# A graph layer with two MLPs on one core: the linear product made first, its scaled rows the gather table

## The chip, the cores and the metric

One Trainium2 chip, one of its cores. The time is the device's, in microseconds, of the whole program; each kernel is run several times and the median is given. The engines are named TensorE (PE in the profile), VectorE (DVE), ScalarE (ACT), GpSimd (POOL) and SyncE (SP). All numbers are fp32.

## The reference

x is 3125 nodes of 256 features; there are 50,000 edges, sorted by destination, with a weight each.

```python
def gnn(features, src, dst, w, W, b):
    msgs = features[src] * w[:, None]
    agg = segment_sum(msgs, dst, 3125)
    return einsum('ni,oi->no', agg, W) + b

x = x + gnn(layernorm(x), src, dst, edge_weight, W, b)
x = x + ffn(layernorm(x))
```

`ffn` is a shared MLP of three layers plus the two best of four small expert MLPs, mixed by a softmax gate. Layer norm subtracts the mean of a row and divides by its deviation.

## The kernel before, in words

The nodes are 25 tiles of 128. At the start each tile of x is loaded (SyncE, line 599), its statistics are made on VectorE (1163), the deviation on ScalarE (758), and the tile is normalised into `xn_all`, three of four tiles on ScalarE (764), one on VectorE (1180). Each group of four tiles is then stored to a table `normalised_rows` in HBM (ScalarE's DMA queue, 739). There are seven groups, and all seven must have landed (`s_table`) before any row is read back.

The sums by destination are made in two ways.

For the first 19 tiles of nodes (units G0 to G10, one or two tiles each) the edges' source rows are gathered from HBM. A chunk is 128 edges. GpSimd issues one indirect DMA a chunk. 12 chunks are a batch, and there are 26 batches, 308 chunks. The first 24 chunks (2 batches, `RAW_BATCHES`) are gathered from x itself, so that they need not wait for the table (692); their rows are normalised in SBUF afterwards (751, 1322). The other 284 come from the table (708), into a ring of three batches. A slot of the ring is free when TensorE has used it (`s_used`). TensorE multiplies each chunk with a selector that VectorE makes (1356, 1360) into a window of 128 node slots (927), ScalarE copies the window (776), and `merge` puts windows in their places in the unit (945) with a placement matrix (1368).

For the last 6 tiles (units D0 to D2) no gather is needed: VectorE makes one-hots from the edges' records, 36 groups of them (1408, 1412), TensorE builds a dense adjacency (962), ScalarE copies it (786), and TensorE multiplies it with `xn_all` (974).

Either sum is features by nodes. ScalarE copies it (`sums`, 801), TensorE multiplies it with the weights W (`lin`, 990), VectorE adds x and the bias (1432) and makes the statistics (1436, 1440). Then a unit goes through std on ScalarE (807), norm (1451), turn (1001), logits and layer 1 (1011, 1025), the gates, layers 2 and 3 (1034 to 1070), `finish` (1544) and the store (652).

After a start that is written out by hand, the order of steps on each engine is made by `schedule()` at build time. It keeps a clock for each engine with assumed durations and picks among the steps that are ready by rank: `FIRST` for batches, `BUILD`, `MULT`, `BEHIND` for a younger unit. All three engines follow its lists, in order. ScalarE changes between a table with square root and one with exp, and each change is a load (ACT_TABLE_LOAD).

Line 700, GpSimd's branch on a flag, stands between the raw gathers and the others; so do branches on the other engines. The flag says that the edges fit the windows; with these inputs they do, and the other branch is never run.

## Time and profile before

| what | us |
|---|---|
| median of 3 runs | 438.74 |
| the three runs | 437.04, 442.10, 438.74 |
| the profiled execution, its own time | 436.16 |
| its span, first to last instruction | 434.4 |
| busy: TensorE / VectorE / ScalarE / GpSimd | 355.3 / 242.1 / 161.8 / 307.4 |
| mean granted clock of TensorE | 0.953 |

A row of the timeline gives start, duration, engine, line, operation, out<-in and how many were merged; in brackets the idle time of the engine before it and what ended it. "issue" means that the profile shows nothing that the engine waited for. A group's row gives its busy time, the mean of one, and the idle time of the engine before it. An fp32 matmul is two records in the profile, a transpose one. The granted clock is a share of 2.4 GHz; 0.5 is 1.2 GHz.

### The profile page before, as it was taken

The page shows a single profiled execution, that of the slowest core. Times are in us where ns is not written, and L with a number is a line of the kernel's source. Part 1 is how long each engine was busy: PE and PEld are TensorE (multiplying, and loading weights), DVE is VectorE, ACT ScalarE, POOL GpSimd, SP SyncE. Part 2 cuts the span into 40 slices and gives each one's busy share as a digit, 9 for nine tenths or more (in the row PEclk, how much of TensorE's full clock was granted, in tenths as well). Part 3 has the DMA queues.
Part 4 walks back from the last instruction along what each step waited for, and adds up shares of the span by engine and source line. Part 5 has one row for each costly group of instructions (what it writes and reads, how often), then busy time and mean ns, then how long its engine had stood idle before and what let it go on. Part 6 is the DMA issues. An engine that isn't in the chain of part 4 may idle for free.

```text
span 434.4 us, 7468 instructions
## 1 busy us (share of the span) xinstructions
PE 355.3 (82%) x2404; PEld 287.5 (66%) x2404; DVE 242.1 (56%) x917; ACT 161.8 (37%) x334; POOL 307.4 (71%) x317
## 2 busy tenths in 40 slices
PE   0004486899999999967999999879999988997885
PEld 0003356688788889655888798669787866874674
DVE  6999838997325789731333459324254463441433
ACT  1634624342323546121313337403225353342352
POOL 7775777877777787777777777777777777777200
PEclk9999658999999999996999999998999999998989
DMA  6995754444454333343343343343343444343200
GB/s 195 366 353 136 197 146 102 101 100 99 108 127 106 97 119 98 91 129 108 102 130 101 107 128 92 102 129 106 103 133 103 123 114 116 110 125 106 72 2 30
DMA packets 48963, 53.32 MB, mean 123 GB/s; under 512 B 27819, under 2 KB 38810, under 8 KB 48922
## 3 DMA queue, kind: packets, MB, share of 16 engines
q0 software_dynamic: 14784, 40.39, 32.1%
q1 hardware_dynamic: 30442, 9.14, 9.0%
q10 hardware_dynamic: 3696, 3.28, 2.2%
q8 instruction: 21, 0.34, 0.3%
q14 instruction: 20, 0.16, 0.1%
HBM read 46.30 MB, written 6.48 MB: 121 GB/s over the span
## 4 chain that ended last, share of the span: by engine, by line
POOL 65%; issue 21%; DMA 5%; PE 4%; DVE 2%; ACT 1%; SPq 1%; POOLq 0%; DVEq 0%
POOL rows L708 65%; DMA x_sb<-in_x 3%; PE hid_ps L1025 1%; SPq L599 1%; DMA rows<-normalised_rows,src_all 1%; PE tok_ps L1067 1%; DMA normalised_rows<-xn_all 1%; PE tok_ps L1065 0%; PE window_ps L927 0%; ACT xn_all L764 0%; DVE stats L1163 0%; PE agg_ps L945 0%; ACT L807 0%; PE mid_ps L1001 0%; POOLq L345 0%
## 5 line engine op out<-in xcount | busy, mean ns | idle before, releaser
L708 POOL DMA_INDIRECT rows<-normalised_rows,src_all x284 | 283.2, 997 | 89.2 <-issue 89.2
L927 PE MATMUL window_ps<-rows,select 128*32 128x256 f32 x616 | 44.5, 424 | 30.7 <-DMA rows<-normalised_rows,src_all 16.4
L974 PE MATMUL agg_ps<-dense,xn_all 128*128 128x256 f32 (+1 forms) x300 | 68.7, 372 | 0.0
L974 PEld LDWEIGHTS agg_ps<-dense,xn_all 128*128 128x128 f32 x300 | 55.2, 198 | 7.8 <-issue 2.6
L927 PEld LDWEIGHTS window_ps<-rows,select 128*32 128x32 f32 x616 | 20.2, 118 | 47.2 <-issue 29.1
L834 ACT ACTIVATE h<-hid_ps,b_sb 128x256 f32<-128x256 f32 (+2 forms) x84 | 32.9, 442 | 42.8 <-PE hid_ps L1025 42.6
L1025 PE MATMUL hid_ps<-xt,ew_sb 128*128 128x256 f32 (+2 forms) x224 | 47.9, 360 | 0.0
L1025 PEld LDWEIGHTS hid_ps<-xt,ew_sb 128*128 128x128 f32 x224 | 39.1, 195 | 5.1 <-issue 1.2
L1356 DVE TENSOR_TENSOR select<-slots,rel 128x384 f32<-128x384 f32 (+1 forms) x26 | 14.2, 544 | 40.1 <-PE window_ps L927 40.1
L1544 DVE TENSOR_TENSOR y<-tok_ps,x 128x512 f32<-128x512 f32 (+1 forms) x14 | 8.9, 634 | 39.5 <-PE tok_ps L1070 39.5
L776 ACT ACTIVATE windows<-window_ps 128x256 f32<-128x256 f32 (+1 forms) x26 | 9.9, 383 | 51.4 <-PE window_ps L927 50.4
L692 POOL DMA_INDIRECT rows<-in_x,src_first x24 | 22.9, 952 | 7.7 <-issue 6.7
L1067 PE MATMUL tok_ps<-ew_sb,h 128*128 128x256 f32 (+1 forms) x100 | 27.4, 399 | 0.0
L962 PE MATMUL build_ps<-high_node,low_1h 128*128 128x125 f32 x144 | 21.5, 296 | 5.2 <-DVE high_node L1412 5.2
L1025 PE MATMUL hid_ps<-xt,sw_sb 128*128 128x256 f32 (+2 forms) x112 | 24.9, 366 | 0.0
L990 PE MATMUL agg_ps<-gnn_wt_sb,sums 128*128 128x256 f32 (+1 forms) x100 | 24.3, 382 | 0.5 <-ACT sums L801 0.5
L962 PEld LDWEIGHTS build_ps<-high_node,low_1h 128*128 128x128 f32 x144 | 19.5, 207 | 7.5 <-DVE high_node L1412 6.2
L1408 DVE TENSOR_TENSOR low_1h<-iota,lo_f 128x512 f32<-128x512 f32 (+1 forms) x36 | 24.1, 671 | 0.0
L1412 DVE TENSOR_TENSOR high_node<-high_1h,node_1h 128x500 f32<-128x500 f32 (+1 forms) x36 | 23.7, 659 | 0.0
L1067 PEld LDWEIGHTS tok_ps<-ew_sb,h 128*128 128x128 f32 (+1 forms) x100 | 19.9, 199 | 3.3
L945 PEld LDWEIGHTS agg_ps<-place,windows 128*128 128x128 f32 (+1 forms) x160 | 20.7, 198 | 2.0 <-ACT windows L776 1.4
L945 PE MATMUL agg_ps<-place,windows 128*128 128x152 f32 (+5 forms) x160 | 20.8, 283 | 0.5 <-ACT windows L776 0.5
(143 smaller groups left out, 565.8 us busy)
## 6 DMA issues: line engine op xcount, KB each, us to landing
rows<-normalised_rows,src_all POOLq DMA_INDIRECT x284, 2.8
x_sb<-in_x SPq DMA_DIRECT2D x6, 512.0 KB, 9.4
normalised_rows<-xn_all ACTq DMA_DIRECT2D x6, 512.0 KB, 7.8
out<-y SPq DMA_DIRECT2D x10, 256.0 KB
records<-in_rec SPq DMA_DIRECT2D x144, 1.5 KB
ew_sb<-in_ew SPq DMA_DIRECT2D x1, 512.0 KB
out<-y SPq DMA_DIRECT2D x4, 128.0 KB
rows<-in_x,src_first POOLq DMA_INDIRECT x24, 5.1
```

The source lines that it names most:

```text
L692: pool.indirect_dma_start(rows[:, b * BATCH + pos, :], None, x[:, :], bass.IndirectOffsetOnAxis(ap=src_first[:, c:c + 1], axis=0)).then_in ...
L708: pool.indirect_dma_start(rows[:, b % RING * BATCH + pos, :], None, table[:, :], bass.IndirectOffsetOnAxis(ap=src_all[:, c:c + 1], axis=0) ...
L834: last = act.activation(u.h1[:, m, 0:tok], by_half(u.hid_ps[k % 2])[:, m % 2, 0:tok], ACT.Relu, bias=b1_sb[:, m:m + 1])
L927: last = pe.matmul(window_ps[SLOT * g:SLOT * (g + 1), 0:D], select[:, b % RING, j, :], rows[:, b % RING * BATCH + pos, :], start=(i == 0), ...
L945: last = pe.matmul(gathered_ps[:, k * PAIR + lo - lo_node:k * PAIR + hi - lo_node], windows[0:full, b % KEEP, k * P:(k + 1) * P], place[0: ...
L962: last = pe.matmul(built_in(k)[:, j * width:(j + 1) * width], low_1h[:, k % RING, j, :], high_node[:, k % RING, j, :, :].rearrange("p h n ...
L974: last = pe.matmul(dense_ps[:, k * PAIR:k * PAIR + tok], xn_all[:, h, k * P:(k + 1) * P], dense[:, h, 0:tok], start=(h == 0 and k == 0), s ...
L990: last = pe.matmul(gathered_ps[0:r, t * D:(t + 1) * D], sums[q % 2][:, k, t * P:t * P + r], gnn_wt_sb[:, k, :], start=(k == 0), stop=(k == ...
L1025: last = pe.matmul(by_half(u.hid_ps[b % 2])[:, m % 2, 0:tok], w, u.xt[:, k, 0:tok], start=(k == 0), stop=(k == KD - 1))
L1067: pe.matmul(o, u.h2[:, 1 + k, c], ew3_sb[:, k, :], start=False, stop=False)
L1408: dve.tensor_tensor(low, iota[:, 0:P].unsqueeze(1).to_broadcast([P, n, P]), lo_f[:, c].unsqueeze(2).to_broadcast([P, n, P]), ALU.is_equal)
L1412: dve.tensor_tensor(high_node[:, r, 0:n, :, :], high.unsqueeze(3).to_broadcast(both), node.unsqueeze(2).to_broadcast(both), ALU.mult).then ...
```

## The change

Layer norm and the linear product are exchanged. Since (x - mean) W = x Wc, where every column of the weights has its mean taken off, LN(x) W is x Wc times the reciprocal deviation. So x Wc is made first, for all 25 tiles, and what goes to the table (and to `xn_all`) is the product with its rows scaled. What is gathered and summed is already the linear step's output.

- The weights are loaded first on SyncE's queue. TensorE sums their columns with a matrix of ones, VectorE takes the mean off (`centre_weights`).
- 13 pairs of tiles (12 of two, one of one): TensorE turns the pair (`turn_x`), ScalarE copies it (`copy_x`), TensorE multiplies (`multiply_x`), ScalarE scales it into `xn_all` (`scale_product`). Lines 764 and 1180 are gone. TensorE's other first steps stand between pairs: counts behind pair 1, bases behind 6, the fault's turn behind 9.
- The sums are now nodes by features: `merge` takes the placement as weights and the window as the moving side, 256 columns each time; the multiplication with the adjacency likewise. `sums` and `lin` are gone, and `residual` reads the sum straight from PSUM. The placement is 256 columns wide instead of 152.
- The 24 raw rows are not normalised. Their reciprocal deviations go into their edge weights (`row_w`), and each of the two raw windows is turned, multiplied with the weights and written back (`turn_raw`, `multiply_raw`) before the merge.
- `RAW_BATCHES` stays at 2. The planner's constants and its assumed start times change, so the order behind the start differs.

```diff
-PARTS, OPEN, BANKS = 4, 3, 2
-NEAR, BEHIND, HURRY, FIRST = .2, 3, 2.0, 0.7
-BUILD, MULT, LATE = 0.4, 1.3, 0.0
+OPEN, BANKS = 3, 2
+NEAR, BEHIND, HURRY, FIRST = .2, 1.2, 3.0, -0.5
+BUILD, MULT, LATE = 6, 1.9, 0.0
...
             sp.dma_start(src_first[:, :], src[:, 0:RAW_BATCHES * BATCH]).then_inc(s_first_src, 16)
+            sp.dma_start(gnn_wt_sb[:, :, :], gnn_wt.rearrange("(k p) n -> p k n", p=P)).then_inc(s_wt, 16)
...
+            def scale_product(p):
+                g, t0, n = pairs[p]
+                r = P if n == 2 else TAIL
+                act.wait_ge(s_product, p + 1)
+                act.wait_ge(s_rstd0, g + 1)
+                for i in range(n):
+                    last = act.activation(xn_all[0:r, t0 + i, :],
+                                          product_ps[p % 3][0:r, i * D:(i + 1) * D], ACT.Identity,
+                                          bias=zero[0:r, :], scale=rstd0[0:r, t0 + i:t0 + i + 1])
                 last.then_inc(s_normed, 1)
+
+            for p, (g, t0, n) in enumerate(pairs):
+                copy_x(p)
+                if t0 == groups[g][0]:
+                    deviations(g)
+                if p:
+                    scale_product(p - 1)
+                    if t0 == groups[g][0]:
+                        store_table(g - 1)
...
+            turn_x(0)
+            for p in range(len(pairs)):
+                if p + 1 < len(pairs):
+                    turn_x(p + 1)
+                multiply_x(p)
+                if p == 1:
+                    count(0)
+                elif p == 6:
+                    edge_bases()
+                elif p == 9:
+                    pe.wait_ge(s_fault, 1)
+                    pe.transpose(u.mid_ps[0:1, 0:P], fault[:, :], ident[:, :]).then_inc(s_fault_t, 1)
...
-            def linear(q, ready, count):
...
+                for t, batches in merges_of(unit):
+                    for b in batches:
+                        full = P if batch_size(b) == BATCH else SLOT * len(quad(b, 0))
+                        at = (unit.tile + t - first_tile(b)) * P
+                        last = pe.matmul(gathered_ps[:, t * D:(t + 1) * D],
+                                         place[0:full, b % KEEP, at:at + P],
+                                         windows[0:full, b % KEEP, :],
+                                         start=(b == batches[0]), stop=(b == batches[-1]))
...
-                dve.wait_ge(s["lin"], n)
+                if aggregated is None:
+                    dve.wait_ge(s_merged if unit.kind == "G" else s_multiplied, unit.i + 1)
+                    aggregated = by_half(gathered_ps if unit.kind == "G" else dense_ps)[:, 0:T, :]
```

TensorE at the program's start, before: column counts, the bases and the fault's turn, and then the branch.

```order
L893 MATMUL window_ps<-smaller_n,ones 128x56
L899 MATMUL tok_ps<-dst_f,top_row 128x104
L902 MATMUL mid_ps<-dst_f,top_row 32x26 x4
L907 MATMUL mid_ps<-ident,fault 1x128
L1073 TENSOR_LOAD flag
```

TensorE at the same place after the change (line 984 sums the weights' columns, 954 turns a pair of x, 967 multiplies it; `h` is where the turned x lies). The first ten rows:

```order
L984 MATMUL tok_ps<-gnn_wt_sb,ones 128x256 x2
L954 MATMUL hid_ps<-ident,x_sb 128x128 x8
L967 MATMUL build_ps<-gnn_wt_sb,h 128x256 x4
L954 MATMUL hid_ps<-ident,x_sb 128x128 x2
L967 MATMUL agg_ps<-gnn_wt_sb,h 128x256 x4
L943 MATMUL window_ps<-smaller_n,ones 128x56
L954 MATMUL hid_ps<-ident,x_sb 128x128 x4
L967 MATMUL agg_ps<-gnn_wt_sb,h 128x256 x2
L954 MATMUL hid_ps<-ident,x_sb 128x128 x4
L967 MATMUL build_ps<-gnn_wt_sb,h 128x256 x4
```

The turns and products stand ahead of the old first steps, and the pattern goes on through pair 12.

ScalarE at the end of the program, before, from the window of the last batch (25) on: G9's xt, ex and relus, G10's sum and std between them (`h<-hid_ps,b_sb` are the relus; the first and the second of layer 1 stand as x4, the third as x2).

```order
L776 ACTIVATE windows<-window_ps 96x256
L815 ACTIVATE xt<-mid_ps 128x2x128
L821 ACT_TABLE_LOAD
L821 ACTIVATE ex<-low 128x4
L801 ACTIVATE sums<-agg_ps 128x2x128
L834 ACTIVATE h<-hid_ps,b_sb 128x128 x4
L826 ACTIVATE gex<-glow 128x4
L834 ACTIVATE h<-hid_ps,b_sb 128x128 x2
L807 ACT_TABLE_LOAD
L807 ACTIVATE std<-mv,eps 128x1
L844 ACTIVATE h<-hid_ps,b_sb 128x128
```

The same place after the change.

```order
L830 ACTIVATE windows<-window_ps 96x256
L865 ACTIVATE xt<-mid_ps 128x2x128
L871 ACT_TABLE_LOAD
L871 ACTIVATE ex<-low 128x4
L884 ACTIVATE h<-hid_ps,b_sb 128x128 x4
L857 ACT_TABLE_LOAD
L857 ACTIVATE std<-mv,eps 128x1
L876 ACT_TABLE_LOAD
L876 ACTIVATE gex<-glow 128x4
L884 ACTIVATE h<-hid_ps,b_sb 128x128 x2
L894 ACTIVATE h<-hid_ps,b_sb 128x128
```

G10's std has moved ahead of G9's gex and third relu, and a second table load stands between them.

## Rows read from the trace of the kernel before

**Rows 1.** The page: span, and engines' shares of the chain that ended last

```profile
span 434.4 us, 7468 instructions
...
POOL 65%; issue 21%; DMA 5%; PE 4%; DVE 2%; ACT 1%; SPq 1%; POOLq 0%; DVEq 0%
```

**Rows 2.** The page's part 5: busy us, mean ns | idle before, releaser

```profile
L708 POOL DMA_INDIRECT rows<-normalised_rows,src_all x284 | 283.2, 997 | 89.2 <-issue 89.2
```

**Rows 3.** The table's tile: duration ns min/median/max, first and last start us

```profile
L708 POOL DMA_INDIRECT rows<-normalised_rows,src_all x284: 942/946/1831, 35.6 to 404.1; - x142
```

**Rows 4.** Timeline, 28 to 37 us: start, duration, engine, line, what, count [idle before]

```profile
29.06 0.37 ACTq L739 DMA_DIRECT2D normalised_rows<-xn_all  x1
...
31.71 0.95 POOL L692 DMA_INDIRECT rows<-in_x,src_first  x1 [0.30 <-issue]
...
34.00 0.34 SPq L630 DMA_DIRECT2D gnn_b_sb<-in_gnn_b  x1
...
35.61 1.25 POOL L708 DMA_INDIRECT rows<-normalised_rows,src_all  x1 [2.95 <-issue]
```

**Rows 5.** Landings: table stores (line 739); the weights' load (KB, median us)

```profile
DMA to landing us min/median/max: 4.9/8.0/9.0
...
gnn_wt_sb<-in_gnn_wt SPq DMA_DIRECT2D x1, 256.0 KB, 3.6
```

**Rows 6.** Timeline of TensorE, 38 to 104 us

```profile
38.08 2.79 PE L927 MATMUL window_ps<-rows,select 128*32 128x256 f32 x24 [10.43 <-ACT rows L751]
40.80 2.07 PE L962 MATMUL build_ps<-high_node,low_1h 128*128 128x125 f32 x8
42.67 1.30 PE L962 MATMUL agg_ps<-high_node,low_1h 128*128 128x125 f32 x8
...
55.63 2.79 PE L927 MATMUL window_ps<-rows,select 128*32 128x256 f32 x24 [3.85 <-issue]
...
98.77 4.91 PE L974 MATMUL agg_ps<-dense,xn_all 128*128 128x256 f32 x22
103.52 0.60 PE L1001 MATMUL mid_ps<-ident,xn 128*128 128x128 f32 x4
```

**Rows 7.** Timeline, 5 to 7 us: VectorE's first statistics of x

```profile
6.14 1.41 DVE L1163 BATCH_NORM_STATS2 stats<-x_sb 128x6 f32<-128x256 f32 x4 [0.97 <-DMA x_sb<-in_x]
```

**Rows 8.** Stretches: length, busy PE, PEld, DVE, ACT, POOL; granted clock, DMA share, GB/s

```profile
10.00:20.00 10.00, 1.62 (x12) 1.13 (x12) 9.38 (x47) 6.10 (x14) 7.56 (x9) 1.00 1.08 368
...
62.00:66.00 4.00, 3.58 (x28) 2.16 (x20) 1.65 (x5) 0.44 (x2) 3.09 (x4) 0.79 0.45 102
```

**Rows 9.** ScalarE's groups by shape: busy us, mean ns | idle before, releaser

```profile
L834 ACT ACTIVATE h<-hid_ps,b_sb 128x256 f32<-128x256 f32 x60 | 25.1, 470 | 35.6 <-PE hid_ps L1025 35.5
...
L815 ACT ACTIVATE xt<-mid_ps 128x512 f32<-128x512 f32 x10 | 6.0, 597 | 19.1 <-PE mid_ps L1001 19.1
```

**Rows 10.** Line 708 in 125 to 185 us, and in 300 to 350 us

```profile
L708 POOL DMA_INDIRECT rows<-normalised_rows,src_all x44 | 46.6, 1059 | 13.4 <-issue 13.4
...
L708 POOL DMA_INDIRECT rows<-normalised_rows,src_all x41 | 39.2, 955 | 12.5 <-issue 12.5
```

**Rows 11.** Timeline of the tail, 407 to 432 us

```profile
407.40 1.49 PE L927 MATMUL window_ps<-rows,select 128*32 128x256 f32 x16 [0.78 <-DMA rows<-normalised_rows,src_all]
...
412.69 0.38 ACT L801 ACTIVATE sums<-agg_ps 128x256 f32<-128x256 f32 x1 [1.46 <-PE agg_ps L945]
...
414.57 0.42 DVE L1432 TENSOR_TENSOR x<-agg_ps,x_sb 128x256 f32<-128x256 f32 x1 [1.65 <-PE agg_ps L990]
...
416.04 1.28 ACT L807 ACT_TABLE_LOAD   x1
...
416.08 0.71 PE L1034 MATMUL hid_ps<-h,sw_sb 128*128 128x128 f32 x4 [0.71 <-ACT h L834]
...
422.27 0.50 PE L1011 MATMUL mid_ps<-gate_w_sb,xt 128*128 128x4 f32 x4
...
431.64 0.34 SPq L652 DMA_DIRECT2D out<-y  x1
```

397 lines of the change are left out of this document (209 added, 188 removed).

## The prediction, made before the changed kernel was run

> **What bounds the kernel now.** I read the chain of work that ended last first. Its shares [rows 1] give GpSimd's gathers (line 708) 65% and "issue" 21%; the two are one thing, because the gathers come in a row with 0.30 us between them. The group of line 708 [rows 2] says it in sums: 284 gathers, 283.2 us busy, mean 997 ns, 89.2 us idle before them, all put down to issue and none to a wait. The tile's view [rows 3] gives the shortest as 942 and the median as 946 ns. So from 35.61, where the first table gather starts, to 405.04, where the last ends (404.1 [rows 3] and 0.95), GpSimd takes 369.4 us for 284 gathers. It never waits for a ring slot, so TensorE is not the bound in that stretch, and work taken off it there is hidden behind the gathers. The time is then three terms: when the first table gather starts, 369.4 us, and the tail from 405.04 to 434.4 (29.4 us). The profiled execution lasted 436.16 us, 1.8 more than its span; the median of the three runs, 438.74, lies 2.6 above it and the lowest, 437.04, 0.9 above.
>
> What sets the first term is in [rows 4]. ScalarE issues the last table store at 29.06, right behind its last tile. SyncE, which waits for the whole table before line 630, goes on at 34.00. That is 4.9 us after the issue, which is also the shortest landing of these stores [rows 5]. GpSimd, done with its 24 raw rows at 32.66, waits for the same semaphore, reads the flag and branches: first gather at 35.61, 1.6 us after 34.00. So of the raw rows' cover only 1.3 us were missing before (32.66 to 34.00).
>
> **Part 1: the start.** Removed: 19 ACTIVATEs of line 764, 6 TENSOR_SCALARs, the shifts. Added in front of every table store: four transposes, one copy of 128x512, four fp32 matmuls and two scalings per pair of tiles, through TensorE and ScalarE in turn. TensorE did next to nothing there before, so this is not hidden: the table waits for it, and GpSimd waits for the table.
>
> Prices at the upper clock level come from [rows 6]: 22 matmul records (an fp32 matmul is two, so 11 of 256 columns) take 4.91 us, 0.433 each when the last one's drain is left out; 4 transposes take 0.60, 0.11 each by the same reckoning. A tile is 2 matmuls and 2 transposes, 1.08 us, and 25 tiles make 27.1 us. At the lower level (1.2 GHz) I double these.
>
> The line of time. The first x load, with nothing in its way, is in use at 6.14 [rows 7]. After the change the weights (256 KB) go ahead of it: 0.4 us of SyncE's issue and about 0.7 us of transfer (256 KB at the 368 GB/s of 10 to 20 us [rows 8]), so 7.2. Two more things come before the first multiply: its turn at the lower level (0.9) and the copy (0.60, line 815, [rows 9], and 0.2 of waits), so 8.9. The column sums and the centring on VectorE run beside these. From 8.9 TensorE's own order counts: products 25 x 0.866 = 21.7; the turns not yet done, 21 tiles x 0.22 = 4.6; the three small steps (counts, bases, fault) 1.0; half speed until about 12, 1.6 more; waits for copies in the first pairs 0.4; and 0.6 for the fault, because VectorE's checks stand behind a reciprocal that now waits for ScalarE's ninth pair. End of the last product: 38.8. ScalarE is not the bound by little: 0.60 + 0.94 for two scalings (line 834, the same shape out of PSUM, [rows 9]), with std and a store every second pair about 1.9 us, against 2.17 of TensorE.
>
> Then 0.2 and 0.94 for the last two scalings, so the last store is issued at 39.9 instead of 29.06. Its landing: 4.9 was the shortest in a stretch where the DMA engines were full [rows 8]; 256 KB took 3.6 in a quieter one [rows 5]. At 40 us the raw rows and the x loads are over, so I take 3.6 + 0.7 = 4.3 and keep 3.6 and 4.9 as ends. Table complete 44.2, first gather 1.6 later, 45.8: **10.2 us later** than 35.61. GpSimd is idle from 32.7. Nothing takes this cover's place: the raw rows are 24 as before.
>
> By the Trainium skill, DMA: Bandwidth & Descriptors, Anatomy of one DMA, a transfer is about 2.0 us fixed and its bytes at 436 GB/s, an estimate of 3.2 us for 512 KB; with it the sum below would be 1.1 us less. This trace shows no store of a table group under 4.9.
>
> **Part 2: the gathers.** The same 284, on the same queue, 369.4 us. VectorE's one-hots, selectors and unit steps stay in number; the placement of line 1368 grows from 152 to 256 columns, 26 times. GpSimd's gathers are 1059 ns in 125 to 185 us and 955 in 300 to 350 [rows 10], so they stretch in some company; 26 wider instructions could stretch a few, four more one-hot groups now run before the first gather. Both are under 2 us; I take 0.
>
> **Part 3: TensorE in the middle.** The linear step of line 990 leaves: 2 matmuls a tile, 50 x 0.433 = 21.7 us. The merges become full 256-column matmuls (about 50, 21 us, against 80 short ones), and two raw batches add 2 turns and 2 matmuls each, 2.2 us. Less work, all behind the gathers: worth 0, and the ring is safer for it. The raw batches' turn, copy, product, copy sit between batch 0 and the first merge; first needed by unit G0, which has over 15 us.
>
> **Part 4: the tail.** Before [rows 11]: batch 25 at 407.40, the sum of G10 copied at 412.69, x1 at 414.57, G10's table load 416.04, layer 2 of G9 at 416.08, logits of G10 at 422.27, last store 431.64. Gone: the copy and the linear step, 1.9 us from 412.69 to 414.57, with x1 of G10 now straight behind the merge. But the order on ScalarE changes too (the order rows of the change): G10's std stands ahead of G9's gex and third relu, with a table load of 1.28 us for the one and another for the other. Layer 2 of G9 waits for that relu. Counted from batch 25's start: the merge ends at 5.2 as before (412.69 less a hair), layer 1b's products 0.9 later, G9's first relus at 6.8 (0.6 for two); then table load to 8.1, std 8.4, table load 9.7, gex 9.9, relu 10.6, so layer 2 at 10.6, where it stood at 8.7 (416.08). Layer 2 and its relus, 1.3 each, end at 13.3, layer 3 starts at 13.8, 2.2 later than before, and logits of G10, queued behind layer 3 on TensorE, come at 15.8 to 17.3 against 14.9. So the tail grows by 1 to 2.4; I take **1.5**. If the relu were not held, it would shrink by 1.9.
>
> **Sum:** 436.16 + 10.2 + 0 + 0 + 1.5 = 447.9. Half the median's distance would add a little and the rounded terms lean long, so 448.
>
> **The rivals.**
> First, a quick start and a shorter tail. The last product ends at 37 (no half speed, no fault wait), the store lands in 3.6, the tail is 1.9 shorter: 448 - 1.8 - 0.7 - 3.4 = 442. For it: the linear step is really on the tail's path before. Against: the first dense stretch of this trace begins at the lower level. 16%.
>
> Second, the clock. From 38.08 TensorE worked without a gap at the lower level for 4.8 us: line 962 takes 2.07 us for 8 records at 40.80 and 1.30 for the next 8 at 42.67 [rows 6], so the pace rose in these, at about 42.9. From 55.63 it took until about 63.7, 8.1 us: the mean granted clock is 0.79 in 62 to 66 [rows 8], that is 1.7 us at half. If the start needs 8 us, or the clock falls again in a wait, each such us costs half of itself or more: 451 to 456, 10%. If it stays at 1.2 GHz for the whole stage, 27 us more, 475; 2%. The Trainium skill, TensorE: Matmul & The Clock Gate, Part 4: PE-mode transpose, says that transposes don't count as activity for the clock; in the new stage they are 0.44 of 2.17 us a pair, so by that rule this rival gains, and the forecast stands only if the products alone are enough.
>
> Third, the ring: with the table late and units crowded behind, a batch on TensorE comes too late and GpSimd waits for a slot. It has never waited before; 3 us would give 451; 5%.
>
> Fourth, the other side: the gathers' stretching goes away. 284 at 946 ns would be 268.7 us instead of 283.2, 14.5 less, 433.5. It must take at least 11.7 us off the gathers for the change not to lose. For it only that one-hots move ahead of the gathers; against it, 32 of 36 groups don't. The Trainium skill, SBUF — State Buffer, tells of a port that VectorE and GpSimd share with a lock, under which a wider placement speaks for longer gathers, not shorter. 3%.
>
> **The numbers.** The forecast itself, 444.5 to 451.5: 64%. About 1% (4.4 us) is what a measurement here can tell from no change, so slower means above 443.1. The first rival lies mostly below it, with the low end of the forecast's unknowns (landing 3.6, start at 37): same 12%, faster 3%, slower 85%. The range from 441.5 to 454 leaves out the fourth rival, the stuck clock, and the far ends of the second and third, under 2 in 10.
>
> **What would show it.** GpSimd: a gap of some 13 us between the last raw row (about 32.7) and the first table gather (45.8), then 284 gathers with 0.30 us between them and no wait for TensorE, about 369 us. TensorE: dense from about 9 to 39, granted clock 1.00 after 12. Last table store near 40. Tail 30 to 32 us. I am wrong if the first table gather starts before 42 or after 49, if GpSimd waits in its ring, or if the gathers take less than 360 us.

## The result, and the profile after

The changed kernel took 457.26 us (median; its profiled execution 457.46, span 455.7), the kernel before 438.74 (434.4 of span). Against the kernel before on the same chip the ratio was 1.040, 95% interval 1.029 to 1.050, and in a later session, with more runs, 1.0456 (1.0418 to 1.0494). It is slower, as forecast, but by 18 to 20 us and not by 10. (In one session, that of four of the experiments below, every kernel took some 600 to 620 us, the kernel before 616; three of the four were run again and carry the ending _r, the fourth is b_twice.)

From the page of the changed kernel: the span, the shares of the chain that ended last, and the groups that answer to [rows 1, 2] (busy us, mean ns | idle before).

```profile
span 455.7 us, 7463 instructions
...
POOL 49%; PE 28%; issue 15%; ACT 3%; DMA 3%; DVE 1%; SPq 0%; POOLq 0%; ACTq 0%
...
L748 POOL DMA_INDIRECT rows<-normalised_rows,src_all x284 | 288.8, 1017 | 99.5 <-issue 99.5
L1080 PE MATMUL agg_ps<-xn_all,dense 128*128 128x256 f32 (+1 forms) x300 | 77.2, 389 | 0.3 <-ACT dense L849 0.3
...
L1052 PE MATMUL agg_ps<-windows,place 128*128 128x256 f32 (+1 forms) x100 | 25.3, 400 | 0.5 <-ACT windows L830 0.5
```

The table's tile in the changed kernel, to be read beside [rows 3]:

```profile
L748 POOL DMA_INDIRECT rows<-normalised_rows,src_all x284: 942/947/2860, 46.0 to 420.1; - x142
```

TensorE had 4% of the chain before and has 28% now. The pieces of that chain in order of time (start, length, what) show where it leaves GpSimd: at 333 us, some 90 us before the last gather.

```profile
332.06 0.95 POOL rows L748
333.01 0.30 issue
333.31 2.85 DMA rows<-normalised_rows,src_all
336.17 0.14 issue
336.30 1.50 PE window_ps L1016 x24
```

The start, in the timeline of the changed kernel (start, length, engine, line, what, count [idle before and what ended it]), to be read beside [rows 4]:

```profile
4.30 2.04 PE L984 MATMUL tok_ps<-gnn_wt_sb,ones 128*128 128x256 f32 x4 [4.30 <-DMA gnn_wt_sb<-in_gnn_wt]
9.22 1.94 PE L954 MATMUL hid_ps<-ident,x_sb 128*128 128x128 f32 x8 [2.88 <-DMA x_sb<-in_x]
11.00 2.85 PE L967 MATMUL build_ps<-gnn_wt_sb,h 128*128 128x256 f32 x8
...
34.28 1.89 PE L967 MATMUL agg_ps<-gnn_wt_sb,h 128*128 128x256 f32 x8
38.38 1.99 PE L967 MATMUL build_ps<-gnn_wt_sb,h 128*128 128x256 f32 x8
...
41.46 0.37 ACTq L778 DMA_DIRECT2D normalised_rows<-xn_all  x1
44.39 0.35 SPq L670 DMA_DIRECT2D gnn_b_sb<-in_gnn_b  x1
46.00 1.20 POOL L748 DMA_INDIRECT rows<-normalised_rows,src_all  x1 [13.28 <-issue]
```

**The loss in four parts.** Cut at the same four events, the two profiled executions give:

| | before | after | difference |
|---|---|---|---|
| first table gather starts | 35.6 | 46.0 | +10.4 |
| 284 gathers, to the end of the last | 369.4 (405.0) | 375.0 (421.0) | +5.6 |
| from there to TensorE's first matmul of batch 25 | 2.4 (407.4) | 5.7 (426.7) | +3.3 |
| from there to the end | 27.0 | 29.0 | +2.0 |
| span | 434.4 | 455.7 | +21.3 |

The first part is what was forecast (10.2), the last one nearly (1.5). The two in the middle were forecast at 0. They are what the experiments are about. (Counted from the last gather's end, as the prediction counts its tail, the last two together are 34.7 us where 29.4 was before.)

TensorE from the first window to batch 25, changed kernel and then before (stretch, its length, busy us of PE, PEld, DVE, ACT, POOL, granted clock, DMA share, GB/s):

```profile
48.00:427.00 379.00, 333.08 (x2116) 250.96 (x2118) 199.49 (x707) 115.52 (x243) 287.08 (x283) 0.94 0.41 111
```

```profile
38.00:407.00 369.00, 333.25 (x2253) 269.95 (x2253) 198.78 (x709) 132.82 (x267) 281.12 (x283) 0.95 0.42 114
```

Its busy time in this stretch is the same to 0.2 us, although the linear step is gone from it.

Where TensorE falls behind can be read batch by batch. In the changed kernel it starts each of batches 3 to 19 but one within 2.4 us of the batch's last gather (batch 8: 4.6) and stands idle 22.1 us in all, waiting for rows. Then it starts batch 20 5.7 us behind, batches 21 and 22 13 us, batch 25 5.6. The jump falls where the multiply of unit D2 stands: its 100 records are the last of line 1080, and from 331 to 385 us TensorE is busy for 52.7 of 54. In the kernel before they ran from 280 to 326 (19.2 us busy for 29.7 after), and batches 21 to 25 start 1.9 to 3.9 us behind their rows. Changed kernel, then before:

```profile
L1080 PE MATMUL agg_ps<-xn_all,dense x100: 379/379/483, 331.0 to 384.4; 128*128 128x256 f32 x50, 128*53 128x256 f32 x50
```

```profile
L974 PE MATMUL agg_ps<-dense,xn_all x100: 317/317/670, 280.1 to 326.3; 128*128 128x181 f32 x100
```

And the start of TensorE's work there, changed kernel, engine by engine:

```profile
51.70 0.67 DVE L1498 TENSOR_TENSOR high_node<-high_1h,node_1h 128x500 f32<-128x500 f32 x1
58.96 0.17 DVE L1462 TENSOR_SCALAR hi_i<-records 128x16 int32<-128x16 int32 x1 [6.60 <-DMA records<-in_rec]
61.41 4.01 DVE L1392 BATCH_NORM_STATS2 row_stats<-rows 128x6 f32<-128x256 f32 x12
68.59 0.56 DVE L1442 TENSOR_TENSOR select<-slots,rel 128x384 f32<-128x384 f32 x1
...
61.55 2.07 PE L1069 MATMUL build_ps<-high_node,low_1h 128*128 128x125 f32 x8 [6.62 <-DVE high_node L1498]
69.80 2.79 PE L1016 MATMUL window_ps<-rows,select 128*32 128x256 f32 x24 [6.18 <-DVE select L1446]
83.05 1.81 PE L1052 MATMUL agg_ps<-windows,place 128*128 128x256 f32 x4
```

VectorE waits 6.6 us for the second block of records, and only behind that takes the statistics of the second raw batch, whose rows GpSimd had finished by 32.7. So TensorE gets the selectors of that batch at 69.80 (55.63 before, [rows 6]), and the first merge, which opens the row of units, comes at 83.05 where in the kernel before it came at 58.91: 24 us later, of which the late table explains 10.

```profile
58.91 1.96 PE L945 MATMUL agg_ps<-place,windows 128*128 128x124 f32 x8 [0.49 <-ACT windows L776]
```

### The profile page after: what moved, and what is told of

It is laid out like the page before. It is cut to its first block, busy times and chain, and to the rows that moved or that the text cites. A ratio compares the mean times of both kernels' runs of the same rounds, so it can differ in the third digit from the quotient of the medians.

```text
span 455.7 us, 7463 instructions
## 1 busy us (share of the span) xinstructions
PE 387.2 (85%) x2410; PEld 294.9 (65%) x2410; DVE 239.3 (53%) x901; ACT 150.8 (33%) x320; POOL 313.3 (69%) x318
## 4 chain that ended last, share of the span: by engine, by line
POOL 49%; PE 28%; issue 15%; ACT 3%; DMA 3%; DVE 1%; SPq 0%; POOLq 0%; ACTq 0%
POOL rows L748 49%; PE agg_ps L1080 6%; PE hid_ps L1116 4%; PE agg_ps L967 2%; PE window_ps L1016 2%; PE tok_ps L1160 2%; PE build_ps L967 2%; PE agg_ps L1052 2%; DMA x_sb<-in_x 2%; PE tok_ps L1158 1%; PE hid_ps L1125 1%; PE hid_ps L1129 1%; PE hid_ps L954 1%; PE tok_ps L1163 1%; PE mid_ps L1102 1%
## 5 line engine op out<-in xcount | busy, mean ns | idle before, releaser
L748 POOL DMA_INDIRECT rows<-normalised_rows,src_all x284 | 288.8, 1017 | 99.5 <-issue 99.5
L1080 PE MATMUL agg_ps<-xn_all,dense 128*128 128x256 f32 (+1 forms) x300 | 77.2, 389 | 0.3 <-ACT dense L849 0.3
L1016 PE MATMUL window_ps<-rows,select 128*32 128x256 f32 x616 | 45.4, 430 | 28.3 <-DMA rows<-normalised_rows,src_all 22.1
L1080 PEld LDWEIGHTS agg_ps<-xn_all,dense 128*128 128x128 f32 (+1 forms) x300 | 49.6, 179 | 21.0 <-issue 15.4
L1016 PEld LDWEIGHTS window_ps<-rows,select 128*32 128x32 f32 x616 | 21.3, 119 | 46.5 <-issue 33.8
L1116 PE MATMUL hid_ps<-xt,ew_sb 128*128 128x256 f32 (+2 forms) x224 | 47.2, 357 | 0.0
L1069 PEld LDWEIGHTS build_ps<-high_node,low_1h 128*128 128x128 f32 x144 | 20.8, 218 | 16.3 <-DVE high_node L1498 15.8
L1116 PE MATMUL hid_ps<-xt,sw_sb 128*128 128x256 f32 (+2 forms) x112 | 28.7, 407 | 0.0
L1617 DVE COPY mix_t<-mid_ps 5x256 f32<-5x256 f32 (+2 forms) x14 | 5.3, 376 | 41.0 <-PE mid_ps L1136 41.0
L1160 PE MATMUL tok_ps<-ew_sb,h 128*128 128x256 f32 (+1 forms) x100 | 26.1, 385 | 0.0
L1052 PE MATMUL agg_ps<-windows,place 128*128 128x256 f32 (+1 forms) x100 | 25.3, 400 | 0.5 <-ACT windows L830 0.5
L1116 PEld LDWEIGHTS hid_ps<-xt,sw_sb 128*128 128x128 f32 x112 | 21.4, 218 | 2.3
L1052 PEld LDWEIGHTS agg_ps<-windows,place 128*128 128x128 f32 (+1 forms) x100 | 19.4, 202 | 5.2 <-ACT windows L830 1.5
## 6 DMA issues: line engine op xcount, KB each, us to landing
x_sb<-in_x SPq DMA_DIRECT2D x6, 512.0 KB, 10.4
```

Source lines behind the costliest of these rows:

```text
L748: pool.indirect_dma_start(rows[:, b % RING * BATCH + pos, :], None, table[:, :], bass.IndirectOffsetOnAxis(ap=src_all[:, c:c + 1], axis=0) ...
L1016: last = pe.matmul(window_ps[SLOT * g:SLOT * (g + 1), 0:D], select[:, b % RING, j, :], rows[:, b % RING * BATCH + pos, :], start=(i == 0), ...
L1052: last = pe.matmul(gathered_ps[:, t * D:(t + 1) * D], place[0:full, b % KEEP, at:at + P], windows[0:full, b % KEEP, :], start=(b == batche ...
L1069: last = pe.matmul(built_in(k)[:, j * width:(j + 1) * width], low_1h[:, k % RING, j, :], high_node[:, k % RING, j, :, :].rearrange("p h n ...
L1080: last = pe.matmul(dense_ps[0:r, t * D:(t + 1) * D], dense[:, h, t * P:t * P + r], xn_all[:, h, :], start=(h == 0 and t == 0), stop=(h == ...
L1116: last = pe.matmul(by_half(u.hid_ps[b % 2])[:, m % 2, 0:tok], w, u.xt[:, k, 0:tok], start=(k == 0), stop=(k == KD - 1))
```

## The experiments

In the names, "a_" stems from the changed kernel, "b_" from the kernel before. Times are ratios to the kernel before on the same chip. Where the constant of the statistics or the planner's start time is changed, the planner also opens the next unit when no engine has anything left to do, since it would otherwise stop. "Over 946" is the gathers' busy time less 0.946 us for each. All columns but the ratio are of one profiled execution. That of b_one_input_r (438.3 us) is the slowest of its ten runs, that of b_half_r (439.1) lies 2.3 us above its median.

| | ratio (95%) | first gather | last gather ends | batch 25 starts | over 946 |
|---|---|---|---|---|---|
| before | 1 | 35.6 | 405.0 | 407.4 | 14.5 |
| after | 1.040 (1.029 to 1.050) | 46.0 | 421.0 | 426.7 | 20.1 |
| a_again | 1.0456 (1.0418 to 1.0494) | 45.9 | 421.2 | 426.8 | 20.3 |
| b_late_table | 1.0064 (1.0039 to 1.0089) | 39.3 | 409.6 | 412.1 | 15.4 |
| a_told | 1.0411 (1.0374 to 1.0448) | 47.2 | 418.3 | 424.2 | 16.2 |
| a_tail | 1.0451 (1.0403 to 1.0499) | 46.3 | 419.9 | 425.6 | 18.6 |
| a_raw36 | 1.0405 (1.0356 to 1.0453) | 49.8 | 416.6 | 424.7 | 19.2 |
| a_stats1 | 1.0351 (1.0305 to 1.0397) | 45.0 | 417.0 | 419.1 | 17.1 |
| a_raw36_stats1 | 1.0344 (1.0270 to 1.0417) | 48.6 | 411.0 | 422.3 | 22.6 |
| a_raw36_s1_half_r | 1.0154 (1.0099 to 1.0209) | 48.8 | 411.8 | 413.7 | 23.1 |
| b_stats4 | 1.0193 (1.0124 to 1.0263) | 35.5 | 410.1 | 412.0 | 19.6 |
| b_half_r | 0.9999 (0.9955 to 1.0042) | 36.1 | 409.9 | 411.9 | 18.8 |
| b_one_input_r | 0.9945 (0.9919 to 0.9971) | 36.0 | 407.2 | 409.5 | 16.3 |
| b_split_high | 1.0051 (1.0014 to 1.0089) | 35.6 | 402.3 | 411.7 | 10.8 |
| a_s1_split | 1.0299 (1.0217 to 1.0380) | 46.6 | 413.8 | 419.7 | 12.3 |
| a_both | 0.9949 (0.9901 to 0.9998) | 49.7 | 399.4 | 401.3 | 9.9 |

### The late table alone (b_late_table)

```diff
             for g, (t0, n) in enumerate(groups):
...
-            store_table(len(groups) - 1)
             row_deviation(0)
             normalise_rows(0, 0, ACT_ROWS)
+            for k in range(3):
+                act.activation(u.h1[:, k, :], x_sb[:, k, :], ACT.Copy)
+            store_table(len(groups) - 1)
```

> The kernel before, with nothing changed but when its last table store is issued: ScalarE does the raw rows' deviation and its 8 raw rows first (they end near 37.9) and three more ACTIVATEs of 256 columns (0.5 us each), so the store goes out near 39.5 instead of 29.06, 10.4 us later, and the table is as late as in the changed kernel. Theory (the four terms of the changed kernel's loss are separate: start +10.4, longer gathers +5.6, last batch late on TensorE +3.2, order in the tail +2.0): only the first comes, first table gather near 46, last gather's end near 415.4, total 438.7 + 10.4 = 449. Rival (a late start also makes TensorE late at the end and the gathers longer, because the order of the work was planned for a table at 35): 455 to 458, the changed kernel's time.

The delay came out a third of what I meant. The timeline of this kernel:

```profile
34.57 0.37 ACTq L739 DMA_DIRECT2D normalised_rows<-xn_all  x1
34.98 3.53 ACT L751 ACTIVATE rows<-rows,row_shift,row_rstd 128x256 f32<-128x256 f32 x7
38.42 1.01 ACT L770 ACTIVATE h<-x_sb 128x256 f32<-128x256 f32 x3
...
39.29 1.85 POOL L708 DMA_INDIRECT rows<-normalised_rows,src_all  x1 [6.02 <-issue]
```

The store stands behind twelve ACTIVATEs in the program, eleven of them behind the last wait for a semaphore, and goes out ahead of ten of them. So the first gather was 3.7 us late, not 10.4. The time grew by 0.64%, 2.8 us (1.7 to 3.9), to 440 and not to 449; the last batch carries none of it (it starts 2.5 us behind the last gather). A late table alone is passed on in the main and not enlarged, which agrees with the first theory at a third of the dose. That a table 10 us late does no more was not run.

### Order: told the true start, the tail, the statistics

```diff
 (a_told)
-        return max(39.5, 4.0 + 1.254 * BATCH * RAW_BATCHES) if b < RAW_BATCHES else land(b)
+        return max(45.5, 4.0 + 1.254 * BATCH * RAW_BATCHES) if b < RAW_BATCHES else land(b)
 (a_tail, behind ORDER, UNITS = schedule())
+LAST_STD = ("std", GATHERED[-1])
+ORDER["act"].remove(LAST_STD)
+ORDER["act"].insert(ORDER["act"].index(("h1", GATHERED[-2])) + 1, LAST_STD)
 (a_stats1; b_stats4 the other way round in the kernel before)
-COUNT_BEHIND, STATS_BEHIND = 4, 4
+COUNT_BEHIND, STATS_BEHIND = 4, 1
```

> The changed kernel with the planner told that the table's gathers begin at 45.5 instead of 39.5; nothing but the order on the engines changes. In its plan unit D2 comes ahead of G7, as in the kernel before, and not behind it. Theory (TensorE starts the last batch 3.2 us late because D2's layers were put late): batch 25 starts about 2.4 us behind the last gather again, 457.3 - 3.2 = 454. Rival (TensorE has more to do than before, in whatever order): no change, 457.

> The changed kernel with one entry of ScalarE's order moved: the std of G10 stands behind the third relu of G9 and not ahead of its gex. Theory (this order makes two table loads of 1.28 us ahead of layer 2 of G9, which is the 2.0 us that the tail grew counted from batch 25): 2.0 us less, 455.3, and more if TensorE then keeps its clock. Rival (something else of the path is then last, such as G10's own std): 457.

> The changed kernel itself, once more, beside the next three and for the three variants of it that came out at 455 to 456 against 436.7 before (told, 36 raw rows, tail). Theory by now (TensorE is late behind GpSimd over the last 100 us, so the end doesn't follow the gathers): it lies where these three lie, 454 to 456, ratio 1.040 to 1.045 to before. Rival (the three gained what they were meant to and the changed kernel is really slower): ratio 1.047 or more.

The times were 455.0, 456.1 and 457.6 us. Neither a_told nor a_tail can be told from a_again: the three intervals overlap, and a_again, at 1.0456, lies just above the theory's 1.045 and below the rival's 1.047. With D2 back ahead of G7 batch 25 still began 5.9 us behind the last gather, so the place of D2 ahead of G7, which I had taken for the cause, is not enough. (Its multiply ran from 316 to 361 us there, 15 to 24 us earlier, and batches 21 and 22 still came 15 us late.) In a_tail layer 2 of G9 did come earlier, 8.1 us behind batch 25 and not 10.5, and G10's own std then came behind a table load of 1.28 us, with another load behind it at 438.58; 1.1 us of it is left in the tail (27.9 against 29.0).

> The changed kernel with one constant of the planner as it was before: VectorE takes the second raw batch's statistics behind the first one-hot group and not behind the fourth, where it first waits 6.6 us for the second block of records (DVE L1462 at 58.96) and only then does them, at 61.41. The planner also moves D1 ahead of G5 and D2 ahead of G7. Theory (TensorE's units begin 19 us later than before, first merge 83.05, 10 of them by the late table and the rest by this order, and the crowd that is pushed back is what makes the last batch late): batch 1's selectors come near 50 and not at 68.6, the first merge near 65 to 70, batch 25 starts 2.4 us behind the last gather, total 455 - 3 to 5 = 450 to 452. Rival (TensorE's total work of the stretch decides, wherever it idles first): 455.

This one is worth 1.0% by the ratios (452.2 us against 457.6; 450 to 452 was expected), and TensorE's timeline shows it:

```profile
56.25 2.79 PE L1020 MATMUL window_ps<-rows,select 128*32 128x256 f32 x24 [0.37 <-DVE select L1450]
63.12 1.10 PE L1056 MATMUL agg_ps<-windows,place 128*128 128x256 f32 x4 [0.68 <-ACT windows L844]
...
419.11 1.49 PE L1020 MATMUL window_ps<-rows,select 128*32 128x256 f32 x16 [3.25 <-DMA rows<-normalised_rows,src_all]
```

The first merge comes 20 us earlier, and batch 25 starts 2.1 us behind the last gather, waiting for its rows and not for TensorE. The +3.3 is gone with the statistics that stood behind a wait for records. But the constant also moved units in the plan (D1 ahead of G5, D2 ahead of G7): D2's multiply now runs from 304 to 352 us, batches 18 to 24 are still 6 to 12.5 us late, and TensorE has made it up by batch 25. The statistics and the place of the units were not taken apart; a_told shows that D2 ahead of G7 by itself does not do it.

> The kernel before with that constant as in the changed kernel: the second raw batch's statistics behind four one-hot groups. Theory (this order alone costs time, also where the table is early): VectorE waits for the second block of records first, near 48, and the statistics, 4.9 us, with all that stands behind them come 10 to 14 us later than before; GpSimd waits in its ring for batch 1's slots near 61 to 66, some 5 us, and the total is 441 to 448. Rival (the slack of TensorE and of the ring absorbs it): 437.

The ratio was 1.019 (1.012 to 1.026), 447.7 us, in the range expected: the same constant costs the kernel before 8 us with its table as early as ever. GpSimd never waited in its ring there, so the place that I had named for the cost is wrong. Nor was batch 25 late (1.9 us behind the last gather). In the profiled execution, the slowest of the four (451.5), the last gather ends 5.1 us later than before and the tail is 37.7 us for 27.0: two sums are copied behind batch 25 where there was one, so more of the units' work is left for the end.

### Closing GpSimd's gap (a_raw36, a_raw36_stats1)

```diff
-RAW_BATCHES = 2
+RAW_BATCHES = 3
```

> The changed kernel with three raw batches: 36 raw rows, 272 table gathers. The raw rows, 1.254 us each, last until about 47.7 and cover the table. Theory (GpSimd's row of gathers sets the time, and the 13.3 us in which it stands idle are the loss): first table gather near 49.2, 272 gathers at 1.30 to 1.32 us end at 403 to 408, and with a tail of 29.4 to 34.6 the total is 434 to 445, most likely 442. Rival (TensorE has become the bound towards the end): earlier gathers only make TensorE later behind them, 450 or more.

> The same with 36 raw rows and 272 table gathers. With 36 raw rows alone GpSimd waited twice in its ring (3.9 us at 70.0, 4.4 at 90.6) since batches 1 and 2 of the raw rows were selected late, and batch 25 still came 8.1 us behind the last gather. Theory (the raw batches' statistics late on VectorE hold TensorE and the ring): no wait in the ring, last gather ends at 403 to 408, batch 25 2.4 to 5 us behind, tail 27 to 29: 434 to 443. Rival (TensorE's work after the table is the bound): 448 to 455.

Both miss: 454.9 and 453.6 us, where 434 to 445 and 434 to 443 were expected; the rivals' ranges hold. With 36 raw rows alone GpSimd waits in its ring, and TensorE is 8.1 us late with batch 25:

```profile
69.96 0.95 POOL L748 DMA_INDIRECT rows<-normalised_rows,src_all  x1 [3.86 <-PE window_ps L1016]
...
90.55 0.94 POOL L748 DMA_INDIRECT rows<-normalised_rows,src_all  x1 [4.40 <-PE window_ps L1016]
...
424.69 1.49 PE L1016 MATMUL window_ps<-rows,select 128*32 128x256 f32 x16
```

With the statistics early as well, the ring is free but for 0.7 us, the last gather ends at 411.0, 6.0 us before that of a_stats1, and batch 25 starts 3.2 us later than there, 11.3 us behind the last gather. The gap of 13 us is closed and nothing is gained. The theory that GpSimd's idle 13 us are the loss falls. Here too TensorE follows its rows within 4.4 us from batch 9 to 19, and is 12 to 18 us late from batch 20 to 22, where D2's multiply stands (327 to 365 us).

### Is TensorE the bound? (a_raw36_s1_half_r, b_half_r)

```diff
             def multiply(v, h):
+                skipped = h % 2 == 1
...
-                for t, r in enumerate(rows_of(DENSE[v])):
+                for t, r in enumerate(rows_of(DENSE[v]) if not skipped else []):
```

> The changed kernel with 36 raw rows and the statistics' constant as before, and of the 75 steps of the D units' multiply on TensorE (line 1080, 73 us in the stretch) only those with an even h: 12 of 25 in each unit are left out, 35 us of TensorE's work, and part of the sums with them. Without this cut the last gather ended at 411.0 and batch 25 began at 422.3. Theory (with 36 raw rows TensorE's own work behind the table is the bound, so that the earlier gathers gained nothing): batch 25 starts within 3 us of the last gather, which ends at 403 to 408, total 434 to 441. Rival (what holds batch 25 is a chain of units through several engines that TensorE's work is no part of): 448 to 454 still.

> The kernel before, and of the D units' multiply (line 974) only the steps with an even h, some 30 us of TensorE's work left out and part of the sums with them. The same cut took 10 us off the changed kernel with 36 raw rows (453.6 to 443.5). Theory (before the change GpSimd's row of gathers is the bound and TensorE has slack): the same 437, at most 2 us less. Rival (TensorE bounds this kernel too): 5 us or more less.

Taking 12 of every 25 multiplies from TensorE makes the changed kernel with 36 raw rows 10 us faster (453.6 to 443.5) and the kernel before no faster at all. (In the second the profiled gathers ended 4.9 us later and the tail was 1.6 shorter, so the equal total alone says little; that batch 25 starts 2.0 us behind the last gather, as before, says that TensorE is not the bound there.) The cut was not run on the changed kernel with its 24 raw rows. In the first, batch 25 now follows its rows:

```profile
413.71 1.49 PE L1020 MATMUL window_ps<-rows,select 128*32 128x256 f32 x16 [0.64 <-DMA rows<-normalised_rows,src_all]
```

The time missed the expected 434 to 441 because the gathers ended at 411.8 and not by 408: these 272 took 1031 ns each. So two rows of work run side by side behind the table: GpSimd's gathers, about 370 us, and TensorE's windows, merges, builds and units, 369 to 378 us with its waits where nothing is cut. Before, GpSimd's was the later one (TensorE waited 16.4 us for rows in all, and 0.78 before batch 25). But TensorE's length is not work alone. In the changed kernel it waits 22.1 us for rows between batches 3 and 19 and is dense only behind 331 us, so what bounds the end is the work that the plan leaves for the last 100 us, D2's multiply above all; the cut takes 14 of its 35 us there. A plan that fills the waits of the middle with that work is the obvious rival to "too much work for TensorE", and none was tried but those of a_told and a_stats1.

### What lengthens the gathers (b_one_input_r, b_split_high, a_s1_split, b_twice)

In the changed kernel's timeline a gather of 1.20 us and one of 0.95:

```profile
45.71 0.67 DVE L1498 TENSOR_TENSOR high_node<-high_1h,node_1h 128x500 f32<-128x500 f32 x1
46.00 1.20 POOL L748 DMA_INDIRECT rows<-normalised_rows,src_all  x1 [13.28 <-issue]
...
258.45 0.69 DVE L1632 TENSOR_TENSOR y<-tok_ps,x 128x512 f32<-128x512 f32 x1 [4.00 <-PE tok_ps L1163]
258.72 0.95 POOL L748 DMA_INDIRECT rows<-normalised_rows,src_all  x1 [0.30 <-issue]
```

The first gather starts 0.29 us into a VectorE product of two SBUF tensors that ends at 46.38; its excess of 0.26 is that end less 0.127 us from its own start. The second starts 0.27 us into an equally long instruction that has one input in PSUM, and pays nothing. I counted the gathers that had a VectorE instruction running from before that point to after it, in nine traces. With high_node's product, 150 of 155 are longer, 118 of them by that amount within 25 ns; with low_1h's 74 of 81. With x1, y and h, each with an input in PSUM, 2 of 149; with the layer norm's statistics, one input, 0 of 96. The exceptions are instructions that start near or behind the gather's own start. Over the sixteen traces of the table, of instructions that had run for 60 ns or more when the gather started and went on 50 ns past the point, every one with both inputs in SBUF made it longer (high_node's 198, low_1h 123, the selectors 92, wide 68), and of 184 with an input in PSUM 2 did. Of 1959 gathers with no VectorE instruction at that point none was longer. TENSOR_SCALARs, with one tensor input, are between: by the same count 31 of 55 in the layer norm, 18 of 24 of 128 columns, 4 of 83 of 32 columns.

That is not all of it. A few gathers are held past the end of the instruction that they met, through others that follow with no idle time. This one of the changed kernel takes 2.86 us, and its excess of 1.91 is the end of the second product (222.88) less 0.127 us from its own start; between the two products shown stand four more instructions, low_1h among them:

```profile
220.66 0.67 DVE L1498 TENSOR_TENSOR high_node<-high_1h,node_1h 128x500 f32<-128x500 f32 x1
220.83 2.86 POOL L748 DMA_INDIRECT rows<-normalised_rows,src_all  x1 [0.30 <-issue]
222.21 0.67 DVE L1498 TENSOR_TENSOR high_node<-high_1h,node_1h 128x500 f32<-128x500 f32 x1
```

The excess of 14.5 us before splits into 11.9 us in 58 gathers that one running instruction explains within 25 ns and 2.8 in 4 that it does not; the 20.1 after into 12.6 in 53 and 7.4 in 10 (10.6 and 9.8 in a_again). So most of the +5.6 lies in a few gathers held for long. Why some are held on and others not (at 46.00 a selector follows the product at once, and the gather went on) stays open.

```diff
-                dve.tensor_tensor(low, iota[:, 0:P].unsqueeze(1).to_broadcast([P, n, P]),
-                                  lo_f[:, c].unsqueeze(2).to_broadcast([P, n, P]), ALU.is_equal)
+                for j in range(n):
+                    dve.tensor_scalar(low[:, j, :], iota[:, 0:P], lo_f[:, c.start + j:c.start + j + 1], None,
+                                      ALU.is_equal)
 (and the selectors: 12 TENSOR_SCALARs, is_equal and mult in one; b_split_high and a_s1_split also:)
-                dve.tensor_tensor(high_node[:, r, 0:n, :, :], ...
+                for j in range(n):
+                    last = dve.tensor_tensor(high_node[:, r, j:j + 1, :, :], ...
```

> The kernel before with two of VectorE's large TENSOR_TENSORs made of instructions with one tensor input: low_1h (line 1408) of four TENSOR_SCALARs of 128 columns, and the selectors (lines 1356 and 1360) of twelve TENSOR_SCALARs of 32 columns that compare and weigh in one. Theory (only VectorE's instructions with two inputs in SBUF hold up a gather's issue): the 4.7 us that lie at these lines go, gathers 365, total 432 to 434. Rival (any VectorE instruction does it, and these are more and together longer): gathers 369 or more, total 437 or more.

> The kernel before with the one-input instructions of the run before for low_1h and the selectors, and the product of line 1412 (128x500, two inputs in SBUF, 0.67 us) cut into four of 128x125. Theory (a gather waits, 127 ns after its start, for the end of a VectorE instruction with two inputs in SBUF, so one of 0.2 us costs next to nothing): the 11.6 us at this line in that run fall to 2 to 5, gathers 361 to 365, total 429 to 432 against 435.2. Rival (four in a row hold the gather as one would): gathers 371, total 435.

> The changed kernel with the statistics' constant as before (452.2 us, gathers 372.0, batch 25 2.1 us behind the last) and with VectorE's instructions as in b_split_high: one-input low_1h and selectors, the product of line 1498 cut into four. Theory (the gathers' excess, 16.8 us there, goes to 5 or less, and TensorE, which had 2 to 4 us of slack left, then becomes last): gathers 360 to 365, total 444 to 449. Rival (the extra time of the gathers is no part of what sets the end): 452.

b_one_input_r is 0.55% faster than the kernel before (435.2 against 437.2), the only complete kernel here that beats both; 432 to 434 was expected. In its profiled execution the gathers did not get shorter: if each longer gather is put down to the instruction that it overlaps longest, what lay at low_1h and the selectors went to 0.3 us, and the product of line 1412 now met 26 gathers and not 19, so that the sum over 946 was 16.3, against 14.5. Its gain is thus not explained by the gathers. Cut in four, that product costs them 2.1 us in place of 11.6 by the same reckoning, but low_1h then has 3.8 in place of 0.3. Put down to the instruction at whose end the gather went on, the product costs 5.9 us in place of 11.2. Either way the sum falls to 10.8, with 5 gathers held through the whole row of four, 0.7 to 0.8 us each, which is what the rival said of all. One of them:

```profile
83.25 1.70 POOL L708 DMA_INDIRECT rows<-normalised_rows,src_all  x1 [0.30 <-issue]
83.25 0.88 DVE L1414 TENSOR_TENSOR high_node<-high_1h,node_1h 128x125 f32<-128x125 f32 x4
```

The page row of b_split_high, and its batch 25:

```profile
L708 POOL DMA_INDIRECT rows<-normalised_rows,src_all x284 | 279.5, 984 | 89.4 <-issue 88.2 <-PE window_ps L927 1.2
```

```profile
411.69 1.49 PE L927 MATMUL window_ps<-rows,select 128*32 128x256 f32 x16
```

The last gather ends 2.7 us earlier than before, and TensorE is 9.4 us late with batch 25: 0.5% slower (439.6 us, where 429 to 432 was expected). VectorE's steps are longer (low_1h 0.87 us for 0.68, high_node 0.88 for 0.67, a selector 2.6 for 1.1), and TensorE waited 14.3 us for selectors where it had waited for rows, so its lateness has a cause of its own. In a_s1_split it is the same (452.0 against 452.2, where 444 to 449 was expected: last gather 3.2 us earlier, batch 25 not). So what holds the gathers is shown by the counts and by the cut, and shortening them this way gains nothing. What shortening them alone would give is not shown, since these cuts also lengthen VectorE's steps.

> The kernel before with VectorE's product of line 1412 (128x500, two inputs in SBUF, 0.67 us, 36 times) done twice in a row into the same place. Theory (a gather's issue that meets such a VectorE instruction waits for its end, which is the 14.3 us that the 284 gathers take over 946 ns each, 20.2 us in the changed kernel; 7.1 of the 14.3 lie at line 1412): about 7 us more in the gathers, 369 to 376, total 442 to 445. Rival (the gathers stretch from something else, such as the DMA rings): gathers 369 to 371, total 437 to 438.

This run took 605 us, beside 616 for the kernel before, and was not repeated. GpSimd waited 127 us in its ring there, so its total answers nothing; in its trace all 58 longer gathers fit the end of the one instruction that they met within 25 ns.

### Both at once (a_both)

a_raw36_s1_half_r with VectorE's steps of a_s1_split.

> The changed kernel with 36 raw rows, the statistics' constant as before, VectorE's one-input and cut instructions, and the D units' multiply (line 1080) only for even h, which leaves out 35 us of TensorE's work and part of the sums. Theory (two rows of work bound it, each of which hides what is gained on the other): the gathers' excess falls from 23 to 9 to 12 us, last gather near 399 to 402, batch 25 within 3 us of it, total 429 to 434, under the kernel before. Rival (something beyond these two holds the end): 440 to 444, as with TensorE's relief alone.

The last gather ends at 399.4 and batch 25 starts 1.9 us behind it, both as expected; the median is 435.6, 1.6 above the expected range, with a tail of 30.6 us that I had not foreseen. It is under the kernel before (0.9949, 0.9901 to 0.9998), but it leaves out 35 us of work that the kernel before does. Relieving TensorE alone gave 10 us, both together 18 (453.6 to 435.6). VectorE's cut instructions alone gave nothing with 24 raw rows (a_s1_split); with 36 they were not run alone.

## Why the prediction was wrong

**The start** (10.2 forecast, 10.4 measured). The sum is right, its pieces are not, and they make up for one another. x was in use at 9.1 and not 7.2, behind the weights' load; the last product ended at 40.4 (38.8), the last store went out at 41.5 (39.9). Against that the store landed in 2.9 us (4.3). The estimate from the Trainium skill, DMA: Bandwidth & Descriptors, Anatomy of one DMA, 3.2 us, was the nearer one, though the section gives its sum for DMAs issued by GpSimd and this store is ScalarE's. TensorE came up to its pace at once (8 records of the first product in 2.85 us, every later 8 in 1.9 to 2.0, granted clock 1.00 from 12 to 41 us), so the clock rival did not come.

**The gathers** (0 forecast, +5.6 measured). "26 wider instructions could stretch a few ... Both are under 2 us; I take 0" is the step that failed. The bound was taken from the number of wider instructions, and those took little (0.2 us, three gathers, by the end that fits). What decides is how many gathers start inside one of VectorE's two-input instructions and are held on through the next ones, and that changes with the order of VectorE's steps against GpSimd's beat of 1.25 us: the kernels of this study that keep those instructions as they are lie between 14.5 and 23.1 us. In the changed kernel 10 gathers were held beyond the instruction that they met (4 before) and took 7.4 us (2.8). The range should have held some 8 us for this. The Trainium skill, SBUF — State Buffer, Who interferes with whom, tells of the lock between such an instruction and a GpSimd operation that reads SBUF, but infers that a tensor_tensor does not hold up descriptor generation; here it holds up the issue of a gather (198 of 198), and the measurement decides. That the coincidences are what lengthened this kernel's gathers rests on the count and on the cut in four; why there were more of the long ones in this order was not traced further.

**TensorE in the middle** (0 forecast, +3.3 measured). Three things failed. The first is "Less work, all behind the gathers: worth 0, and the ring is safer for it". I took 21.7 us off for the linear step and set the merges' growth against it, but left out that the D units' multiply now moves 256 columns for D2's tile of 53 rows: 68.7 us became 77.2. With the merges (20.8 to 25.3) and the raw batches (3.9, forecast 2.2) 16.9 of the 24.3 us that line 990 took are back; layer 1 and the logits make up most of the rest, with no more work to do (+3.1 and +1.8 us, granted clock 0.94 for 0.95), and TensorE's busy time is 333 us in both. The second is that the planner's constant STATS_BEHIND, 4 in place of 1 (the change has it, the lines shown of it leave it out), did not enter the sum at all: "The raw batches' turn, copy, product, copy sit between batch 0 and the first merge; first needed by unit G0, which has over 15 us". What stood before them on VectorE was a wait of 6.6 us for records. a_stats1 shows it, with the units that it moves, to be worth 4.6 to 5.4 us, the 3.3 and part of the longer gathers. The third is that "behind the gathers: worth 0" took the ring as the only way in which TensorE could cost: D2's multiply, 29.7 us of TensorE's time for 19.2 before, ended at 385 us where it had ended at 326, too near the last gather to be made up. The third rival named units "crowded behind" but looked for them in GpSimd's ring, at 3 us. GpSimd never waited there, and they were seen in the lateness of batches 20 to 25.

**The tail** (+1.5 forecast, +2.0 measured). Right in size and in place, if it is counted from batch 25. Batch 25 of the changed kernel starts at 426.67, layer 2 was forecast 10.6 us behind it and came 10.5 behind:

```profile
426.67 1.49 PE L1016 MATMUL window_ps<-rows,select 128*32 128x256 f32 x16
...
433.47 1.28 ACT L857 ACT_TABLE_LOAD   x1
...
435.08 1.28 ACT L876 ACT_TABLE_LOAD   x1
...
437.15 1.22 PE L1125 MATMUL hid_ps<-h,sw_sb 128*128 128x128 f32 x4 [3.46 <-ACT h L884]
...
443.65 0.51 PE L1102 MATMUL mid_ps<-gate_w_sb,xt 128*128 128x4 f32 x4
```

The two table loads stand where the order rows had them, and logits of G10 come 17.0 us behind batch 25 (15.8 to 17.3 forecast). But the forecast took batch 25 as if it followed the last gather as closely as before: its own sign, a tail of 30 to 32 us behind the last gather, failed with 34.7.

The forecast failed most of all by its frame: it found one bound and priced everything behind it at nothing. The row of 38 to 407 us above could have been asked for before: TensorE busy for 333 of 369 us. That TensorE was not the bound before is borne out (b_half_r); that it stays so with the new order was assumed. The first gather, the gap of 13.3 us before it and the ring without a wait came as forecast; that the whole came out slower was forecast for a right reason, the late table, which is about half of the loss.

## What to carry to other kernels

When two engines' rows of work start from one event and are of like length, moving the event can cost both, covering the gap of one may gain nothing, and each gain has to be checked against the other row's end. Look also at where in the other row the work stands: an engine that waits in the middle can still be late at the end. Read "worth nothing, it is hidden" off the second longest row: its busy time plus its own waits, from its own start. And a moved constant in an order table is to be priced by what stands in front of the moved step, which may be a wait.

## What the runs showed that I had not expected

- A gather's issue on GpSimd waits, 127 ns after its start, for the end of a running VectorE instruction with both inputs in SBUF (150 of 155), and not for one with an input in PSUM (2 of 149); now and then it waits on through those that follow, up to 2.7 us (a_stats1). TENSOR_SCALARs are between (4 of 83 of 32 columns, 31 of 55 in the layer norm).
- A DMA issued from ScalarE's queue went out at 34.57 with ten ACTIVATEs in front of it still to run, until 39.4. Here compute placed ahead of a DMA in program order did not delay it.
- The last store of 512 KB landed in 2.9 us at 41 to 44 us, where the shortest of the same size in the full stretch before was 4.9 [rows 5].
